# Local transformer: value and output weights multiplied together per layer, probabilities divided before the weighing

## The reference, cut to what matters

```python
qkv = x @ Wqkv                      # Wqkv: 128 x 3072
q, k, v = heads(qkv)                # q and k: l2norm, scale, rotary
sim = einsum('bhwie,bhwje->bhwij', bq, bk2) * 8.0   # 32 queries, 64 keys
attn = softmax(where(mask, -max, sim), -1)
out = einsum('bhwij,bhwje->bhwie', attn, bv2)       # per head, 64 wide
x = x + out.transpose(0, 2, 1, 3).reshape(b, n, 1024) @ Wo   # Wo: 1024 x 128
x = x + ffn(layernorm(x))           # 128 -> 2 x 341, GELU gate, -> 128
```

## Time and profile before

| | |
|---|---|
| median of 3 runs | 2629.45 us (2624.45 to 2632.44) |
| the profiled execution: span from first to last instruction | 2628.2 us (the page gives no other time for it) |
| busy share of the span: TensorE, VectorE, ScalarE, GpSimd | 93%, 82%, 77%, 58% |
| DMA queue of the program | 275280 packets, 194.42 MB |
| granted clock of TensorE, mean | 0.983 |

### The profile page before, as it was taken

One profiled execution on the slowest core, in us unless ns is written; L12 is line 12 of the kernel. 1 busy time (PEld: TensorE's weight loads), 2 busy tenths in 40 slices (PEclk: granted clock), 3 DMA queues, 4 the chain that ended last, 5 costly groups with the idle time before them and its releaser, 6 DMA issues. The chain is left out here.

```text
span 2628.2 us, 118567 instructions
## 1 busy us (share of the span) xinstructions
PE 2456.8 (93%) x52349; PEld 1960.1 (75%) x52349; DVE 2154.0 (82%) x2455; ACT 2036.8 (77%) x4077; POOL 1516.6 (58%) x1029
## 2 busy tenths in 40 slices
PE   6799999999999999999999999689999999997999
PEld 2478788888887888888888887467776776775787
DVE  5788888888888888888888887388888888885888
ACT  4688888888888889888888887566666666764676
POOL 3788887889778878888887775122322232322111
PEclk8899999999999999999999999799999999999999
DMA  3243434343334344434433333122222222221221
GB/s 96 54 95 92 107 75 94 92 105 81 94 89 104 78 97 98 106 84 95 97 94 81 84 83 72 36 54 52 59 61 58 53 58 59 57 56 31 82 73 41
DMA packets 275793, 202.01 MB, mean 77 GB/s; under 512 B 117568, under 2 KB 215880, under 8 KB 274248
## 3 DMA queue, kind: packets, MB, share of 16 engines
q1 hardware_dynamic: 275280, 194.42, 30.8%
HBM read 36.96 MB, written 1.11 MB: 14 GB/s over the span
## 5 line engine op out<-in xcount | busy, mean ns | idle before, releaser
L512 POOL TENSOR_TENSOR lt_t_sin<-lt_qk,lt_tab 128x512 f32<-128x512 f32 x384 | 684.7, 1804 | 249.5 <-DVE lt_qk L1290 247.4
L517 POOL TENSOR_TENSOR lt_qr<-lt_qr,lt_t_sin 128x1024 f32<-128x1024 f32 x192 | 455.8, 2374 | 28.2 <-POOL lt_t_sin L512 0.9
L2072 DVE TENSOR_REDUCE fa_neg_max<-bank 128x1 f32<-128x1024 f32 x256 | 301.6, 1220 | 94.2 <-PE bank L1869 92.4
L1895 PE MATMUL bank<-fa_prob_t,fa_v 32*64 32x128 f32 x16384 | 294.5, 276 | 19.2 <-issue 14.2
L1994 ACT ACTIVATE fa_prob<-bank,fa_neg_max 128x1024 f32<-128x1024 f32 x128 | 142.5, 1114 | 218.2 <-DVE fa_neg_max L2072 165.9
L1895 PEld LDWEIGHTS bank<-fa_prob_t,fa_v 32*64 32x64 f32 x16384 | 244.4, 130 | 81.2 <-issue 60.9
L2082 DVE STREAM_TRANSPOSE fa_prob_t<-fa_prob 128x1024 f32<-128x1024 f32 x256 | 302.2, 1219 | 0.0
L605 PE MATMUL bank<-lt_w_high,lt_x_high 128*128 128x512 f32 x576 | 278.6, 484 | 0.8 <-ACT lt_v_tok L1005 0.4
L622 PE MATMUL bank<-ident,lt_qr 128*128 128x128 f32 x1536 | 232.0, 275 | 11.2 <-POOL lt_qr L517 7.4
L973 ACT COPY lt_qk<-bank 128x512 f32<-128x512 f32 x384 | 226.5, 591 | 18.5 <-POOL lt_t_sin L512 3.8
L1283 DVE TENSOR_REDUCE lt_ssq<-lt_qr 128x32 f32<-128x2048 f32 x96 | 219.0, 2281 | 25.7 <-ACT lt_qr L981 25.7
(11 more groups left out here) (260 smaller groups left out, 5935.8 us busy)
## 6 DMA issues: line engine op xcount, KB each, us to landing
lt_v<-lt_v_tok SPq DMA_DIRECT2D x576, 128.0 KB
fa_v<-fa_v_tok SPq DMA_DIRECT2D x256, 128.0 KB
lt_v<-lt_v_tok SPq DMA_DIRECT2D x192, 64.0 KB
lt_k_t<-lt_k_t SPq DMA_DIRECT2D x84, 128.0 KB, 2.7
lt_v<-lt_v SPq DMA_DIRECT2D x168, 64.0 KB, 2.2
lt_w_raw<-in_lt_wqkv_dram SPq DMA_DIRECT2D x36, 256.0 KB, 3.4
ex_cw_all<-cw_kept SPq DMA_DIRECT2D x8, 1024.0 KB, 4.6
lt_x_s<-h_in SPq DMA_DIRECT2D x96, 64.0 KB, 2.6
```

Source lines behind the costliest of these rows:

```text
L512: pool.tensor_tensor(dst[:, :, i, :], src[:, :, 1 - i, :], tab[:, g // 2 % 2, 1, at:at + 32].unsqueeze(1).to_broadcast([P, HEADS, 32]), AL ...
L517: pool.tensor_tensor(qr[:, g % 2, half], qr[:, g % 2, half], t_sin[:, :], ALU.add).then_inc(S.rotated, 1)
L1895: mm = pe.matmul(bank[d, 4 + a, 0:P].rearrange("p (u r) -> p u r", u=UPQ), v[rows, half % 2, kb, d], prob_t[rows, q % 2, par, :, 32 * kb:3 ...
L2072: dve.tensor_reduce(neg_max[:, u % 2, par:par + 1], bank[:, 2 * par:2 * par + 2, :].rearrange("p a n -> p (a n)"), AX.X, ALU.max, negate=T ...
```

## The change

- Per layer, TensorE transposes the value weights (`turn_v`, in step 16L-12), VectorE copies them out (`empty_v`), TensorE multiplies them with Wo head by head (`fold`, step 16L-2), ScalarE and VectorE split the product into a high and a low part (`round_fold`, `fold_low`). For layer 0 this is in steps -4 and -2.
- Instead of `project_v` (two blocks of 512 columns) `project_u` forms four blocks: x times U_h for 16 heads, 128 columns each.
- `load_u` moves 128 instead of 64 columns per head, from one buffer (`u_tok`) instead of two, so `empty_u` of a slot waits until the loads of the slot before have landed.
- The probabilities are divided in SBUF before they are transposed (`divide_probs`); `turn_prob` waits for that. In even steps `turn_prob` comes after the third `project_u`, in odd steps after the second.
- `weigh_u` adds all heads up in PSUM: two banks of 128 columns (one for each parity of heads). `add_halves` adds them, one transpose (`turn_att`) brings the sum to features, and `add_residual` takes it from there. `norm_att`, `empty_att` and `project_out` are gone.
- Row sums, division and `add_residual` of the slot before stand ahead of `shift_scores` in every step.
- To make room: `w_o`, `w_1`, `w_2`, `prob_t`, `row_sum`, `ssq` and the raw rotary tables have fewer buffers, and are loaded later or in pieces (`load_tab`, per pair of slots); w_high and w_low hold 6 blocks instead of 10, and 4 blocks per layer are split instead of 6.

```diff
 def load_u(g):
-    sp.wait_ge(S.v_out, 2 * (g + 1))
+    sp.wait_ge(S.u_out, 4 * (g + 1))
...
 if live(i + 1):
-    load_v(i + 1)
+    load_u(i + 1)
...
+def project_u(g, n):
+    wait_free(pe, "u", g, n)
+    if g % SLOTS == 0:
+        pe.wait_ge(S.u_low, 4 * (g // SLOTS) + n + 1)
+    project(g, bank[:, turn_bank("u", g, n), :], u_high[:, n, :], u_low[:, n, :]).then_inc(S.u_proj, 1)
...
+def fold(layer, n):
+    par, q = heads_of(n)
+    f = slice(HD * par, HD * par + HD)
...
+    for m in range(4):
+        hp = 4 * q + m
+        mm = pe.matmul(bank[:, turn_bank("fold", layer, n), m * P:(m + 1) * P], wv_t[f, hp, :], w_o[f, hp, :],
+                       start=True, stop=True)
+    mm.then_inc(S.fold, 1)
...
 def turn_prob(g, n):
     if n == 0:
-        pe.wait_ge(S.probs, 2 * (g + 1))
+        pe.wait_ge(S.divided, g + 1)
...
-                mm = pe.matmul(bank[WIN * w:WIN * w + WIN, value_bank(g, par), hp * HD:(hp + 1) * HD],
-                               prob_t[f, g % 2, hp, WIN * w:WIN * w + WIN],
-                               v[f, g % 2, w, hp, :], start=True, stop=True)
+                mm = pe.matmul(bank[WIN * w:WIN * w + WIN, value_bank(g, par), 0:P],
+                               prob_t[f, hp, WIN * w:WIN * w + WIN],
+                               u[f, g % 2, w, hp, :], start=hp == 0, stop=hp == PAIRS - 1,
+                               skip_group_check=True)
...
-def project_out(g):
...
+def turn_att(g):
+    pe.wait_ge(S.av_out, g + 1)
+    wait_free(pe, "att", g, 0)
+    pe.transpose(bank[:, turn_bank("att", g, 0), 0:BLK], att(g), ident[:, :]).then_inc(S.att_turned, 1)
...
+def empty_u(g, n):
+    par, q = heads_of(n)
+    if g >= 1 and n == 0:
+        act.wait_ge(s_u[(g - 1) % 2], 8 * 16 * ((g - 1) // 2 + 1))
+    act.wait_ge(S.u_proj, 4 * g + n + 1)
+    act.copy(u_tok[:, par, q * CH:(q + 1) * CH], bank[:, turn_bank("u", g, n), :]).then_inc(S.u_out, 1)
...
+def divide_probs(g):
+    dve.wait_ge(S.inv_sum, g + 1)
+    p = prob[:, g % 2, :, :, :].rearrange("p h a k -> p (h a) k")
+    dve.tensor_tensor(p, p, row_sum[:, :].unsqueeze(2).to_broadcast([P, HEADS, HD]), ALU.mult)\
+       .then_inc(S.divided, 1)
...
+def add_halves(g):
     dve.wait_ge(S.av, g + 1)
...
+    dve.tensor_reduce(att(g), bank[:, lo:hi + 1:hi - lo, 0:P].rearrange("p b n -> p n b"), AX.X, ALU.add)\
+       .then_inc(S.av_out, 1)
...
 # VectorE, per step
-if live(i - 1) and even(i - 1, 5) is None:
+if live(i - 1):
     sum_probs(i - 1)
+    divide_probs(i - 1)
+if live(i - 2):
+    add_residual(i - 2)
 if live(i):
     shift_scores(i, 0)
```

More of the change, by code:

```diff
@@ L274, in time_mixing_and_local @@
                 uses["att", i - 2, 0] = len(uses)
[L275 to L286, removed]
+            for n in range(4):
+                if live(i - 1) and n == 2 + (i + 1) % 2:
+                    uses["prob", i - 1, 0] = len(uses)
+                    uses["prob", i - 1, 1] = len(uses)
+                if n == 3 and even(i, 6) is not None:
+                    uses["down", even(i, 6), 0] = len(uses)
+                if live(i + 1):
+                    uses["u", i + 1, n] = len(uses)
+            if folded_at(i) is not None:
+                uses["fold", folded_at(i), 0] = len(uses)
+                uses["fold", folded_at(i), 1] = len(uses)
             if even(i, 5) is not None:
@@ L424, in _ @@
                     load_scale(0, n)
[L425 to L428, removed]
+                load_tab(0)
+                load_tab(1)
+                load_w_o(0)
+                load_vec(0)
+                load_w_1(0)
+                load_w_2(0)
                 for k in range(2, WCH):
@@ new lines, in turn_v @@
+                def turn_v(layer, q):
+                    if q == 0:
+                        pe.wait_ge(S.v_raw, 32 * (layer + 1))
+                        pe.wait_ge(T.ident, 16)
+                    wait_free(pe, "v", layer, q)
+                    for n in range(4):
+                        mm = pe.transpose(bank[:, turn_bank("v", layer, q), n * P:(n + 1) * P],
+                                          v_raw(layer)[:, (4 * q + n) * P:(4 * q + n + 1) * P], ident[:, :])
+                    mm.then_inc(S.v_turned, 1)
@@ L1272, in _ @@
                         square(even(i, 4))
-                    for k in splits_at(i):
-                        if k % WCH >= 4:
-                            split_high(k)
+                    if i >= 0 and folded_at(i) is not None:
+                        for n in range(4):
+                            round_fold(folded_at(i), n)
             @blk.vector
@@ L1531, in _ @@
                 receive(3)
+                empty_v(0, 0)
+                empty_v(0, 1)
                 group_norm(2)
+                for n in range(4):
+                    fold_low(0, n)
                 add_output(2)
@@ L1578, in _ @@
                     if live(i - 1):
[L1579 removed]
+                        add_halves(i - 1)
                     if even(i, 5) is not None:
@@ L1584, in _ @@
                         last_scale(2)
-                    if live(i - 2) and i - 2 < ALL - 1:
-                        add_residual(i - 2)
-                    if live(i - 1):
-                        norm_att(i - 1, 1)
+                    if i >= 0 and v_turned_at(i) is not None:
+                        empty_v(v_turned_at(i), 0)
+                        empty_v(v_turned_at(i), 1)
+                    if i >= 0 and folded_at(i) is not None:
+                        for n in range(4):
+                            fold_low(folded_at(i), n)
                 dve.wait_ge(S.ff_out, CHUNKS)
```

406 lines of the change are left out of this document (228 added, 178 removed).

## The result

The changed kernel takes 2910.7 us (median of 4 runs) where the kernel before took 2627.0 beside it: a ratio of 1.1065 (95% interval 1.1044 to 1.1086), 284 us slower. The profiled execution spans 2899.8 us. From the first transposes of turned queries and keys in its first step to those in its last step (93.2 to 1899.3 us; before, 91.0 to 1621.4) the local transformer now takes 1806 us instead of 1530, and 6 less come after it. This stretch is called the stage from here on. So the whole loss lies in the stage.

The account below looks back on a forecast made before the run. The prediction took TensorE (96% busy) as the bound, with waits through VectorE deciding: 2628 + 89 (pairs) + 20 (folding) + 6 (start) - 3 (end) = 2740 us; own range 2695 to 2785, all cases 2615 to 2800.

Parts of the forecast that it names:

- the chain through VectorE: Local transformer's step pair, from odd weighing's end through normalisation, division and transposes: 34.1 us instead of 32.2, +89 over 47 pairs.
- the 2740: Forecast time of the whole changed kernel in us, given a chance of 0.50.
- the forecast's own range: 2695 to 2785 us for the whole kernel, around the main forecast.
- The division's price: divide_probs between exponentials and turn_prob: 1.2 us, plus 0 to 2.4 waiting for GpSimd at the SBUF port.
- 20 us for the foldings: Folding stretches an even step by up to 4.5 on TensorE, partly in idle time: 4 x 5 = 20.
- the sum took 2.1: Weighing on TensorE, 128 passes of 128 columns: 2.1 us instead of 1.41, +0.7 per step.
- the landing: load_u's bytes arrive 10.0 us after the weighing, before empty_u needs them; costed at nothing.
- the division's lateness: In odd steps the late division hides the loads' landing; without this cover they would cost about 0.5 a pair.
- The cover of 10.9: The odd step's empty_u comes 10.9 us behind the even weighing before waiting for loads costs anything.
- the rival of late loads: DMAs need 13 us, not 10; empty_u 2 us late in every odd step: +2.1 x 47, about 2840; chance 0.08.
- the stalls for issue: TensorE's 24 us of idle for issue in the weighing, expected to fall mostly into time it waits anyway; given nothing.

Follow-up runs that it names:

- the half-byte kernel: The changed kernel, but from the third slot on loads and look-backs carry only four of eight head pairs: 2753.7 us, ratio 1.0473.
- the half-byte kernel with copies: The changed kernel with half of the loads' bytes, plus a 1 MB DRAM-to-DRAM copy behind every step's loads: 2806.9 us, ratio 1.0671.
- the kernel before with copies: The kernel before, plus a 1 MB DRAM-to-DRAM copy behind every step's loads, for which no engine waits: 2806.5 us, ratio 1.0676.

## Why the prediction was wrong

**What was right.** The direction, and the chain through VectorE: in the pair shown every time up to the second division fits within 0.3 us, and the kernel whose loads are out of the way has the pair of 34.15 that was forecast. Its 2753.7 stand 14 over the 2740, within the forecast's own range. The division's price, port wait included, is confirmed from both sides (82 us without it, 46 with one operand in PSUM), and 20 us for the foldings. The Trainium skill's rule (SBUF — State Buffer, Who interferes with whom), that such a division and a GpSimd instruction with an SBUF read shut each other out, agrees with these rows (1.80 to 1.22 and 2.77 to 2.37). An unbroken weighing takes 2.03, where the sum took 2.1, as in this row of the half-byte kernel:

```profile
711.51 2.03 PE L775 MATMUL bank<-lt_u,lt_prob_t 64*32 64x128 f32 x128
```

The Trainium skill's rule on the overhead of matmuls (TensorEngine Tiling (Array Packing), Instruction Overhead), by which the weighing would take 2.82, does not agree with that row.

**What failed first: the landing.** "So I cost this at nothing; its cover is the division's lateness". The prediction had 10.0 us from the weighing to the landing, 8.8 of bytes and 1.2 of lead; the median of the odd steps is 12.8, and 12.9 in the 40 of them whose loads have look-backs. In these 40, by the medians of the trace, all three terms were short. *Bytes:* from the weighing to the landing the engines move 2.42 MB and not 2.1, because other loads that SP issues around them, such as those of tokens, keys and tables, share the engines; at 239 GB/s that is 10.1. *Lead:* SP issues one copy after another, until 7.9 behind the weighing, and in the first four microseconds 0.50 MB go where 0.96 would at 239 GB/s; 1.9 is lost by that, not 1.2. *Pace:* from there to the landing 215 GB/s are moved and not 239, another 0.9. Together that is 12.9. (The pair shown is one of the few without look-backs: it moves 2.09 MB in its 12.6, but starts more slowly still, with 0.35 MB in four microseconds.) The cover of 10.9 was about right: in the pair shown TensorE has turned the probabilities 11.0 behind the even weighing (729.75 and 1.09) and then waits 2.23 for the copy. So the mechanism is the rival of late loads, which was given 0.08, with 13 us and +100: the changed kernel lies 104 above the half-byte kernel with copies, its own traffic without the wait (1.1065 less 1.0671, of 2629).

**What failed second: the stalls.** Of the stalls for issue the prediction said "I give nothing for them", because TensorE waits anyway. Yet they grow with the traffic, and they fall into scores and weighing (L745, L774), which VectorE and the end of the step wait for. They were not hidden: with the copies the half-byte kernel's idle for issue rises by 35 us in the stage, its other waits give back only 5, and TensorE is busy 22 us longer for the same instructions (1495 against 1474), with the clock at 0.50 for 55 us instead of 12. Together that is the 52 us.

The account in parts of the ratio: without division and with half of the bytes +0.0161 (42 us; 20 are the foldings, and TensorE's largest idle left there, 55 us, is the wait for the turned queries behind the odd step's tail on ScalarE), division +0.0312 (82), traffic +0.0198 (52), late landing +0.0394 (104); together 0.1065. Of the last two, part is the clock: TensorE is busy 57 us longer in the stage than with half of the bytes (1530 against 1474), for the same instructions; the clock stands at 0.50 for 121 us of it, against 12. The copies run from DRAM to DRAM and stand behind the loads, so the split between traffic and landing is as good as their likeness to the loads; their sum, 156, is measured by the bytes alone.

## What to carry to other kernels

When bytes are moved between tiles, work out the landing from the first issue on, with the time that one queue needs to fill the engines, and compare it with the buffer's next writer in microseconds: here a landing at 10.0 would have been hidden behind 10.9, and the measured 12.8 was not. Count with it what else the same queue moves in that time. A pause costs more than its length when TensorE comes out of it at half clock. And traffic for which nobody waits is not free for an engine that eats hundreds of small instructions: ask what it does to idle for issue.

## What the runs showed of the hardware that was not expected

- TensorE's instructions come in packets of 16 KB over the DMA engines that also move the data. With 1 MB more per step, for which no compute engine waits, its idle for issue went from 38 to 155 us and the kernel before became 6.8% slower.
- After 3.0 us without matmuls (726.9 to 729.9) the granted clock went to the 1.2 GHz level, and it was still there at 732 to 734. So a stall is paid twice: in the stage of the kernel before with copies, TensorE is idle 112 us longer and, for the same instructions, also busy 58 us longer (1524 against 1467), with the clock at 0.50 for 134 us instead of 16.
- With one operand in PSUM, an elementwise product of VectorE over 128x1024 took 1.22 us on average beside a busy GpSimd, against 1.80 with both in SBUF.
